# The expert up-projection as two single-pass products of 128 rows in a transformer block on one Trainium2 core

## What is computed

```python
h = _layernorm(x) * (1 + ca) + sa
x = x + ga * attention(h, Wq, bq, Wk, bk, Wv, bv, Wo, bo)
h = _layernorm(x) * (1 + cb) + sb
# the experts: E = 4, rank R = 16
logits = flat @ router_w.T                       # top 2, softmax over these: gates
mid = jnp.einsum('tf,erf->ter', flat, A)
all_deltas = jnp.einsum('ter,eor->teo', mid, B) * LORA_SCALE
delta = jnp.einsum('te,teo->to', gates, all_deltas)
x = x + gb * delta
```

## Time and profile before

| | |
|---|---|
| median of 3 runs | 3394.81 us |
| fastest and slowest run | 3388.82 and 3395.46 us |
| span of the profiled execution | 3394.3 us |
| TensorE busy | 3129.1 us, 92% |
| VectorE busy | 1525.6 us, 45% |
| ScalarE busy | 1060.2 us, 31% |
| GpSimd busy | 1138.8 us, 34% |
| mean granted TensorE clock | 0.95 of full speed |

### The profile page before, as it was taken

How to read it: one execution, slowest core, us unless ns; L and a number is a source line. 1 busy time by engine, 2 the same in 40 slices (tenths; PEclk the granted TensorE clock), 3 DMA queues, 4 the chain that set the end, 5 groups by cost and what they waited for, 6 DMA issues and landing times. The chain is left out here.

```text
span 3394.3 us, 53212 instructions
## 1 busy us (share of the span) xinstructions
PE 3129.1 (92%) x17940; PEld 2091.0 (62%) x17940; DVE 1525.6 (45%) x2742; ACT 1060.2 (31%) x1442; POOL 1138.8 (34%) x700
## 2 busy tenths in 40 slices
PE   4999899999989987999999999999999959999997
PEld 2888788778878874444444444444444427677675
DVE  5111221221221115656565565656566425666654
ACT  2223212221121111444444444444444531121110
POOL 3222322332241113434344444434344422332331
PEclk7999999999999996999999999999999979999997
DMA  5444333333324438443434444444344044344341
GB/s 212 186 152 166 146 124 124 124 148 124 124 113 184 173 138 173 101 101 84 97 80 100 98 101 98 101 92 98 82 97 93 14 136 138 101 135 137 99 137 50
DMA packets 149260, 405.35 MB, mean 119 GB/s; under 512 B 16845, under 2 KB 52101, under 8 KB 148057
## 3 DMA queue, kind: packets, MB, share of 16 engines
q1 hardware_dynamic: 149000, 402.95, 40.3%
q10 hardware_dynamic: 80, 0.03, 0.0%
HBM read 271.20 MB, written 131.20 MB: 119 GB/s over the span
## 5 line engine op out<-in xcount | busy, mean ns | idle before, releaser
L861 DVE TENSOR_REDUCE part_max<-ps_r 128x1 f32<-128x128 f32 (+1 forms) x1488 | 802.8, 557 | 553.4 <-PE ps_r L912 365.2
L843 ACT ACTIVATE prob<-ps_s 128x1024 f32<-128x1024 f32 (+3 forms) x768 | 616.0, 811 | 738.7 <-PE ps_s L927 662.0
L909 PE MATMUL ps_r<-k_st,q_st 96*128 96x256 f32 (+1 forms) x1488 | 595.8, 412 | 37.2 <-DMA v_sb<-v_tok 28.3
L609 PE MATMUL ps_u<-h_hi,w_hi 128*128 128x512 f32 x1536 | 603.9, 393 | 0.0
L609 PE MATMUL ps_u<-h_lo,w_hi 128*128 128x512 f32 x1536 | 599.3, 390 | 0.0
L609 PE MATMUL ps_u<-h_hi,w_lo 128*128 128x512 f32 x1536 | 599.3, 390 | 0.0
L909 PEld LDWEIGHTS ps_r<-k_st,q_st 96*128 96x128 f32 x1488 | 287.7, 193 | 455.5 <-DVE part_max L861 390.8
L424 POOL TENSOR_TENSOR w_lo<-w_raw,w_hi 128x1024 fp32r<-128x1024 f32 x96 | 231.0, 2407 | 842.9 <-ACT w_hi L471 842.9
L927 PE MATMUL ps_s<-q_st,k_st 97*128 97x512 f32 (+2 forms) x1536 | 467.6, 387 | 35.5 <-issue 25.5
L546 DVE SCALAR_TENSOR_TENSOR qk_lo<-ps_u,bias_col,qk_hi 128x512 fp32r<-128x512 f32 x128 | 96.1, 751 | 672.0 <-ACT qk_hi L447 672.0
L447 ACT ACTIVATE qk_hi<-ps_u,bias_col 128x512 fp32r<-128x512 f32 x128 | 88.2, 689 | 870.7 <-PE ps_u L609 856.0
(11 more groups left out here) (154 smaller groups left out, 2912.0 us busy)
## 6 DMA issues: line engine op xcount, KB each, us to landing
q_st<-qk_split SPq DMA_DIRECT2D x96, 512.0 KB, 7.5
k_st<-qk_split SPq DMA_DIRECT2D x96, 512.0 KB, 13.7
w_raw<-w_cols SPq DMA_DIRECT2D x72, 512.0 KB, 3.5
qk_split<-qk_hi SPq DMA_DIRECT2D x64, 512.0 KB, 2.7
qk_split<-qk_lo SPq DMA_DIRECT2D x64, 512.0 KB, 3.4
xn<-in_L_attn_x SPq DMA_DIRECT2D x8, 2048.0 KB, 12.2
v_tok<-v_out SPq DMA_DIRECT2D x32, 512.0 KB, 2.7
wm<-in_L_wmod SPq DMA_DIRECT2D x8, 2048.0 KB, 9.0
```

Source lines behind the costliest of these rows:

```text
L609: last = nc.tensor.matmul(ps_u[u % 2][:], w[:, m, k], h[:, k, tok], start=k == 0 and j == 0, stop=k == KT - 1 and j == 2)
L843: nc.scalar.activation(prob[:, k % PBUF, 2 * pair:2 * pair + 2, off:], ps_s[pair][:, :, off:], ACT.Exp, scale=SCALE).then_inc(score_free, 1)
L861: nc.vector.reduce_max(part_max[:, h * TT + i, ch:ch + 1], bank[:, 0:width], AX.X).then_inc(row_free, 1)
L909: last = nc.tensor.matmul(bank[:, 0:cols], q_st[slot][0:QK_ROWS, h, i * P:(i + 1) * P], k_st[slot][0:QK_ROWS, h, ch * BANK:ch * BANK + col ...
```

## The change

The middle is split like the projection's operands: VectorE writes a head in fp32r (`mid_hi`), and then head and rest side by side into `mid_split` (two times 64 columns). The transposes turn all 128 columns, and `mid_t` holds 128 rows: heads above, rests below. `up_hi` holds the head of `up_t` twice, one above the other, so that one product multiplies head and rest of the middle by the head of the weights. `up_lo` holds the rest of `up_t` above and zeros below, so that a second product adds head times rest. Both are made once, at the head of `finish`: the head by ScalarE, its second copy by a DMA within SBUF on SP's queue, the rest by GpSimd. TensorE waits for them before its first projection.

```diff
-        mid_t = sb("mid_t", [ER, CW])
+        mid_hi = sb("mid_hi", [P, T, ER], F32R)
+        mid_split = sb("mid_split", [P, T, 2, ER])
+        mid_t = sb("mid_t", [2 * ER, CW], F32R)
+        up_hi = sb("up_hi", [2 * ER, D], F32R)
+        up_lo = sb("up_lo", [2 * ER, D], F32R)
...
+            sp.wait_ge(up_hi_done, 1)
+            sp.dma_start(up_hi[ER:2 * ER, :].bitcast(F32), up_hi[0:ER, :].bitcast(F32)).then_inc(up_copied, 16)
             sp.dma_start(bo_bc[:], bo.rearrange("(o d) -> o d", o=1).to_broadcast([P, D])).then_inc(bc_loaded, 16)
             load_res(0, 0)
...
+            nc.gpsimd.memset(up_lo[:].bitcast(F32), 0.0).then_inc(up_lo_done, 1)
+            pool.wait_ge(up_lo_done, 1)
+            pool.wait_ge(up_hi_done, 1)
+            nc.gpsimd.tensor_tensor(up_lo[0:ER, :], up_t[:], up_hi[0:ER, :].bitcast(F32), ALU.subtract).then_inc(up_lo_done, 1)
...
+            nc.scalar.copy(up_hi[0:ER, :], up_t[:]).then_inc(up_hi_done, 1)
...
-                nc.vector.tensor_tensor(mid[:].rearrange("p t (e r) -> p t e r", e=E), down[:, :, 0:ER].rearrange("p t (e r) -> p t e r", e=E),
-                                        gate[:].unsqueeze(3).to_broadcast([P, T, E, R]), ALU.mult).then_inc(mid_ready, 1)
+                chain.link(nc.vector.tensor_tensor(mid[:].rearrange("p t (e r) -> p t e r", e=E), down[:, :, 0:ER].rearrange("p t (e r) -> p t e r", e=E),
+                                                   gate[:].unsqueeze(3).to_broadcast([P, T, E, R]), ALU.mult))
+                chain.link(nc.vector.tensor_copy(mid_hi[:], mid[:]))
+                nc.vector.tensor_copy(mid_split[:, :, 0], mid_hi[:].bitcast(F32)).then_inc(mid_ready, 1)
+                nc.vector.tensor_tensor(mid_split[:, :, 1], mid[:], mid_hi[:].bitcast(F32), ALU.subtract).then_inc(mid_ready, 1)
...
-            GATES = 11
+            GATES = 13
...
-                nc.vector.tensor_copy(mid_t[:], ps_l[0:ER, CW:CW + CW]).then_inc(mid_t_ready, 1)
+                nc.vector.tensor_copy(mid_t[:], ps_l[:, CW:CW + CW]).then_inc(mid_t_ready, 1)
...
-                wait_apart(pe, mid_ready, n + 1, tally)
+                wait_apart(pe, mid_ready, 2 * (n + 1), tally)
                 for a in range(T):
-                    last = nc.tensor.transpose(ps_l[0:ER, CW + a * P:CW + (a + 1) * P], mid[:, a], ident[:])
+                    last = nc.tensor.transpose(ps_l[:, CW + a * P:CW + (a + 1) * P], mid_split[:, a].rearrange("p s r -> p (s r)"), ident[:])
...
-                    nc.tensor.matmul(ps_d[u % 2], mid_t[:, a * P:(a + 1) * P], up_t[:, hv * BANK:(hv + 1) * BANK], start=True, stop=True).then_inc(d_done, 1)
+                    nc.tensor.matmul(ps_d[u % 2], mid_t[:, a * P:(a + 1) * P], up_hi[:, hv * BANK:(hv + 1) * BANK], start=True, stop=False)
+                    nc.tensor.matmul(ps_d[u % 2], mid_t[:, a * P:(a + 1) * P], up_lo[:, hv * BANK:(hv + 1) * BANK], start=False, stop=True).then_inc(d_done, 1)
...
             pe.wait_ge(wo_lo_done, KT + 2)
+            pe.wait_ge(up_copied, 16)
+            pe.wait_ge(up_lo_done, 2)
             project(0, 0, 0)
```

More of the change, by code:

```diff
@@ L1092, in finish @@
         mid_turned, mid_t_ready = sem("mid_turned"), sem("mid_t_ready")
+        up_hi_done, up_copied, up_lo_done = sem("up_hi_done"), sem("up_copied"), sem("up_lo_done")
         d_done, d_free, out_ready, out_stored = sem("d_done"), sem("d_free"), sem("out_ready"), sem("out_stored")
```

## The result

The changed kernel takes 3403.01 us in the median of 14 runs (3399.41 to 3408.41), the kernel before beside it 3392.07 us (14 runs, 3387.65 to 3399.64). The ratio is 1.0030, with a 95% interval of 1.0021 to 1.0039: 10.2 us slower, 7 to 13. The profiled execution of the changed kernel has a span of 3402.0 us (3394.3 before).

The account below looks back on a forecast made before the run. It took a ring of VectorE, GpSimd and the res load, not TensorE, as the bound. 15.2 + 0.1 - 2.6 - 1.2 - 1.8 = +9.7 us gave 3404.5 us, 0.3% slower; bounds 3398 to 3413, range with rivals 3398 to 3418.

Parts of the forecast that it names:

- The ring: Last stage, each chunk: VectorE 23.0, GpSimd 4.4, res load by DMA 8.0 us; 35.4 us a round, no TensorE.
- The split: Gates on VectorE: linked mid, two copies and a subtraction add 0.95 us a chunk, +15.2 us over 16.
- `mid_t` with 128 partitions: VectorE's copy of mid_t, same 256 elements on 128 partitions: its 0.41 us stays unchanged.
- (a): Kernel's end: cheaper products of the last up-projection bring the last delta sooner, -2.6 us (2.2 to 3.0).
- (b): Chunk before the last: VectorE's 1.99 us wait for the down-projection shrinks, -1.2 us (0.8 to 1.99).
- (c): Late chunks: addition to res stretched by GpSimd's late splitting, at 2982.34 and two or three others; -1.8 us (0 to 2.7).
- The preparation: Head of the last stage: making up_hi and up_lo costs nothing under the loads of Wo; at worst 1.8 us.
- Rival B: TensorE's clock drops in the wait for mid; 1 to 1.5 us per such chunk, about 3418; 15 in 100.
- A: Last stage: TensorE is the bound after all, so the change gains 26 us, to 3369; 5 in 100.
- C: Up-projection: a single-pass pair costs what the fp32 pair did, credits gone, +15.3 us, 3410; 3 in 100.

Follow-up runs that it names:

- the second pair: Both kernels run once more unchanged, one execution each, for a second trace: kernel before 3396.49 us, changed kernel 3414.84 us.
- the first experiment: Changed kernel with the one-instruction mid of the kernel before, the middle's rest left out: 3388.14 us, ratio 0.9988 to the kernel before.

## Why the prediction was right

- *The ring sets the pace, and TensorE keeps up beside it.* Right. The rounds went from 35.54 to 36.63 us while TensorE had 28 us less to do, and 30 us more for it cost nothing measurable in the changed kernel. The prediction was a little too sure for the kernel before, where TensorE's time costs a third of its length.
- *The split, 0.95 us a chunk.* Right: +0.94 or 0.95 between `mid` and `mid_t` in fourteen rounds, and 1.30 in one. The links cost the 0.15 us that the pair of the earlier trace rows showed (0.23 us of the cast, the next after 0.37). The copies were the cheap kind (0.23 us, against 0.28 for the subtraction), as the two small operations of the earlier trace rows had it and as the Trainium skill (VectorE: DVE Perf Modes, Mode 2×_2P) says of one source within SBUF.
- *`mid_t` with 128 partitions, left at 0.41.* Right, 0.42.
- *(a) The end, -2.6 us.* Right in kind, and 0.3 short: 5.14 instead of 8.03 us, where I had 5.4. The products of a pair are 0.43 us apart at half clock.
- *(b) The chunk before the last, -1.2.* 1.45 in the first pair of traces, where the wait of 1.99 us is gone altogether, and nothing in the second pair, where the kernel before hadn't it. Such a wait is in two of the five traces with fp32 products (one of them has the split, 1.81 us) and in none of the seven with single-pass products.
- *(c) The late chunks, -1.8.* 1.25, and in one chunk alone; in the second pair in two chunks. The prediction's "two or three other chunks" was a misreading: its trace has one more stretched addition, of 1.32 us. The mechanism was only half right too. With the cheap products alone the two additions take 1.42 and 1.41 us, but with the vector work alone, with full fp32 products, they take 1.31 and 1.40. So a later VectorE removes the stretch as well as an earlier TensorE does, and in the changed kernel the two can't be told apart.
- *Missed: the last down-projection.* The sum has no term for it. It brought 2.5 us in the first pair, since it took 4.98 us and not 7.10, and 1.7 in the second (5.37 and 7.09). As kernels with fp32 products have the short one too, this is luck as far as is shown, not the change's doing.
- *The preparation, at nothing.* Right: 90.0 us from the reciprocal to the first `mid` in both. GpSimd's subtraction was running when the reciprocal started, and didn't hold it up:

```profile
2753.01 2.33 POOL L1210 TENSOR_TENSOR up_lo<-up_t,up_hi 64x1024 fp32r<-64x1024 f32 x1
...
2753.60 1.75 DVE L1363 RECIPROCAL inv<-inv 128x256 f32<-128x256 f32 x1 [62.39 <-DMA inv<-att_sum]
```

- *Rival B, the slow clock in a worse place.* Its place was right and its price wrong. The clock fell behind the wait for `mid` in nine of thirteen rounds. But the price is nothing in two of them, 0.13 to 0.36 us in the other seven and 1.5 us in all, where I had 1 to 1.5 us for each. The term mis-sized is the loss: I let the projection end 2 to 3 us late. The stretch at half clock is 3.4 us long and loses 1.7, and about 1.5 of that was covered. The Trainium skill (TensorE: Matmul & The Clock Gate, HAM oscillation) has the pattern, waits that bring the slow clock back round after round. The trace agrees with it in nine rounds of thirteen, though the waits of the skill's example are longer than the 2.1 to 2.6 us here, so that the skill didn't make B "the usual case", as the prediction has it. Here the cover makes the falls cheap.
- *Rivals A and C.* Both fell: A by the first experiment (-4.1 instead of -26), C by the products 0.23 us apart at full clock (3036.56, 3036.79).

So +9.7 foreseen and +10.2 measured come from the same mechanism, the split in the ring, but the closeness of the two is partly luck: the credits change from trace to trace, the slow clock and the late landing (+2.9) were not in the sum, and neither was the last down-projection (-2.5). They nearly cancel.

What stays open is the late landing. One load of `res` lands 9.1 to 9.5 us after GpSimd's end, where the others take 7.5 to 8.3. It is in the traces of all ten other kernels or repeats (in the second round in nine of them, in the thirteenth in the one with fillers in the changed kernel; two have a second one near the end) and in neither of the two traces of the kernel before. Even the one that only moves the copy of `mid_t` has it, which touches neither a transfer nor SP. In the changed kernel, GpSimd and then VectorE:

```profile
2900.55 4.39 POOL L1233 TENSOR_TENSOR delta<-delta,res 128x1024 f32<-128x1024 f32 x1 [2.12 <-DVE delta L1350]
```

```profile
2914.33 0.69 DVE L1303 TENSOR_TENSOR res<-res,att_y 128x512 f32<-128x512 f32 x1 [8.85 <-DMA res<-in_L_attn_x]
```

That is 9.39 us from 2904.94. The loads of the attention that run beside it do so in the other rounds as well, without a loss. What it meets there wasn't found.

## What to carry to other kernels

Ask of an edit which ring it lengthens and not which engine it relieves: an engine that is busy for 92% of the span kept up beside a ring of another engine, a transfer and a third engine, so 26 us less of its work brought about 4 us, while three more small instructions in the ring cost their full 0.95 us each time round. Where a cheaper form on the busy engine needs preparation, put the preparation on an engine outside the ring: on ScalarE and GpSimd, where the copy of `mid_t` went too, it turned a loss of 10 us into a gain of 5. Moving the copy alone, without the cheaper form, gave 4, so what the cheaper form itself added there is too little to tell. Then see which helper works beside the ring, because a helper's small operation beside a wide one of the ring stretched it from 0.69 to 1.10 us.

## What the runs showed of the hardware that was not expected

- A short operation on other partitions than its neighbours had a longer pitch than its duration tells. The subtraction of 64x256 lasts 0.43 us and takes 1.18 us from the start ahead of it to the start behind it (3023.57 to 3024.75). The copy of 128x256 lasts 0.42 us and takes 0.95 (3030.37 to 3031.32). The subtraction and the operation behind it each start 0.03 us after the one ahead has ended, where the copy and its successor start 0.08 us before that. Why is not shown. That one operand lies in PSUM isn't enough, since two `delta` multiplications of 0.69 us, which have that too, take 1.28 together. What sets the subtraction apart is that it also waits for ScalarE, and that it works on partitions 64 to 127 while its neighbours start at partition 0.
- The place where the granted clock falls follows the waits. It fell within the up-projection before the change, behind the wait for `mid` after it, and in the up-projection again once that wait was filled with work. It didn't fall behind every such wait: it followed nine, of 2.1 to 3.7 us, and not two others, of 2.19 and 2.37 us. Each stretch behind that wait was about 3.4 us at 1.2 GHz and lost about 1.7 us of TensorE's time, nearly all of it covered.
- At the end of the kernel the last down-projection of 32 products took 7.10 us at half clock (granted 0.50) and 4.98 us where its first 2 us ran at full clock, a difference of 2.1 us in the path that ends last. Both kinds occur with either form of the products.
- Of a VectorE addition and a GpSimd subtraction that meet, the one that starts second is stretched: 1.10 instead of 0.69 us for the addition, 1.11 instead of 0.74 us for the subtraction.
- One load, mostly that of the second round, landed about 1.4 us late in ten traces of twelve, for a reason that stays open.
